# Cross attention written out straight: half of a subtraction on ScalarE, score products side by side, keys and the quantiser's last steps on GpSimd

## The chip, the cores and the metric

The program runs on one NeuronCore of one Trainium2 chip. A core has TensorE (PE: matmuls and transposes, with weight loads shown apart as PEld), VectorE (DVE), ScalarE (ACT), GpSimd (POOL) and SyncE (SP, which here only starts transfers). Every engine works through its own list of instructions in order, and semaphores join the lists. The metric is the device time of the whole program in microseconds (us); lower is better. Three runs of the kernel before gave 5644.22, 5659.84 and 5665.61 us.

## The reference, cut to what matters

The program is a chain of eight parts over x (32 sequences of 128 tokens of 128 features). The change is in the seventh, a cross attention between `seq1` = x and `seq2` = a side input, with 16 heads of 8 features:

```python
query = seq2 + b_self
key   = concatenate([seq1 + b_prev, seq2 + b_self], 1)
value = concatenate([seq1, seq2], 1)
q, k, v = query @ Wq + bq, key @ Wk + bk, value @ Wv + bv     # split into 16 heads of 8
score_prev = einsum("bhqd,bhkd->bhqk", q, k[:, :, :l1]) * SCALE
score_self = (q * k[:, :, l1:]).sum(-1, keepdims=True) * SCALE
score_prev = where(arange(l1) < seq_len1, score_prev, -inf)
weights = softmax(concatenate([score_prev, score_self], -1), axis=-1)
attn = weights[..., :-1] @ v[:, :, :l1] + weights[..., -1:] * v[:, :, l1:]
return attn @ Wo + bo
```

Each query so sees the 128 tokens of `seq1` and, of `seq2`, only its own token. What comes out is then brought to a 4-bit grid (blocks of 16 values with one 8-bit scale each, `fake_quant_nvfp4`) for the last part.

## The kernel before, in words

The layer is `level3_cond`, a block of five instruction lists. Its unit is one sequence, 32 in all, and its work is laid out by the helper `pipeline`, which gets an engine and a list of pairs (function, lag). In slot `s` the helper issues each function of the list, in the list's order, for the unit `s` minus lag. So the order of a list is the order in which an engine meets its work in a slot, and the lags say which sequence each piece is for. Before, the first slots are written out, then a loop (`Fori`) of 8 slots runs over the middle ones, then the last slots are written out.

For one sequence the work is this. TensorE projects four sequences at once (`project`: q, k, k of seq2, v by turns, one for each slot) and, with x as weights, makes the values and the own scores (`values_in`, into `m_ps`). `scores` multiplies queries by keys for 8 of the 16 heads (`half` 0 and 1) into `s_ps`; the keys lie in `k4` as four copies, in each of which all heads but one of a group of four are zeroed by the mask `hm` (function `keys`). VectorE takes the maximum over a row (`row_max`), joins it with the own score (`less_max`, first instruction) and subtracts it (`z_`). ScalarE takes the exponential (`p`), TensorE turns it (`turn_p`), ScalarE copies the turned weights out (`pT`, `keep_p`), and TensorE forms numerator and denominator in `o_ps` (`values`, 64 small products). ScalarE copies the own weight (`own_weight`, tile `owe`), GpSimd multiplies it with the own value (`own_value`, tile `tt`), VectorE divides (`join`, four instructions: `den`, `rec`, `num`, `att`), TensorE projects (`output`), and VectorE adds the bias (`finish`, into `y_tm`). All parts of `o_ps` lie in one PSUM bank: `values` of a sequence waits for `yc`, the signal of `finish` for the sequence before it.

```python
                def values(k, j, c):

                    pe.wait_ge(s_["yc"], at(k - 1))
                    pe.wait_ge(s_["owe"], at(k))
```

Once in four sequences VectorE quantises 128x512 numbers: `block_scales`, `block_values`, `block_bins` and `block_round`, 15 steps and a last product, spread over four slots by the lags 8, 9, 10 and 11. `keys` (lag 2), `shift` (two additions, lag 0) and `products` (GpSimd, lag 2) too come once in four slots.

Of the kernel before, what the change touches and what calls it, by code (L numbers as in the profile page):

```python
# [24 lines left out]
P = 128  # L25
# [39 lines left out]
def pipeline(eng, units, period, stages, k0=0, first=None, last=None, early=()):  # L65
# [3 lines left out]
    lag = max(g for _, g in stages)  # L69
    head = -(-lag // period) * period  # L70
# [1971 lines left out]
def level3_cond(nc, T, R):  # L2042
# [5 lines left out]
    with ExitStack() as ctx:  # L2048
# [25 lines left out]
        vz = m.sb("ca_vz", [P, 2, GT])  # L2074
# [4 lines left out]
        z_ = m.sb("ca_z", [P, 2, 2 * GT])  # L2079
        p = m.sb("ca_p", [P, 2, 2 * GT])  # L2080
        pT = m.sb("ca_pT", [P, 4, GT])
# [20 lines left out]
                 "top", "topo", "z", "ex", "ownz", "owe", "pT", "pTc", "oweT", "od", "owec", "t", "den", "rec",  # L2102
                 "num", "att", "y", "yc", "xstep", "xq")
# [5 lines left out]
        def diagonal(c):  # L2109

            a = vz[:, c % 2, :]
            return bass.AP(a.tensor, a.offset, [a.ap[0], [4 * 32, 4], [32 + CD, 4], [1, CD]])

        with nc.Block() as block:
            @block.sync
            def _(sp):
# [15 lines left out]
                pipeline(sp, B, 2 * GS, [(load, 0)])  # L2132

            @block.gpsimd
            def _(pool):
                m.credit(pool)
                pool.memset(vz[:, :, :], 0.0).then_inc(s_["init"], 1)
# [20 lines left out]

                def own_value(k, j, c):
# [5 lines left out]
                pipeline(pool, B, 2 * GS, [(copy_x, 0), (products, 2), (own_value, 6)])  # L2165

            @block.tensor
            def _(pe):
# [27 lines left out]
                def scores(k, c, half):  # L2196
# [3 lines left out]
                    pe.wait_ge(s_["z"], at((k - 1) * 2 + half))  # L2200
# [12 lines left out]
                def turn_p(k, c, g):  # L2213
                    pe.wait_ge(s_["ex"], at(k * 2 + g // 2))
# [6 lines left out]
                def values(k, j, c):  # L2221
# [638 lines left out]
```

## Time and profile before

| | |
|---|---|
| median of 3 runs (lowest, highest) | 5659.84 us (5644.22, 5665.61) |
| the profiled execution's own time | 5666.48 us |
| its span | 5664.7 us, 139636 instructions |
| busy over the whole span | PE 4998.9 (88%), DVE 3738.3 (66%), ACT 3349.9 (59%), POOL 3134.2 (55%) |
| the layer that is changed | from about 5091.5 to 5482.6 us in the span, 391.1 us |

The span is the time from the first to the last instruction of the profiled execution; what lies around it is 1.8 us. The changed layer is 391.1 us of it, about 7%. A busy share over the whole span says little of this layer, which is why the views below are all taken inside it. An engine's busy time counts its instructions; idle time that stands behind an instruction in brackets is what the engine waited just before it, with the instruction that ended the wait.

### The profile page before, as it was taken

What the parts mean: (1) busy time and instruction counts of PE and PEld (TensorE: products, weight loads), DVE (VectorE), ACT (ScalarE), POOL (GpSimd) and SP (SyncE); (2) the same over time, 40 slices, a digit from 0 to 9 for tenths busy, and PEclk for the clock granted to TensorE, in tenths of its full rate; (3) what the DMA queues carried; (4) which work ended last, traced back from release to release, by engine and by line L of the source; (5) the groups of instructions that cost most, each with busy time, mean ns of one, the idle gap of its engine ahead of it and who ended that gap; (6) DMA issues with size and microseconds to landing.
All of it is one profiled execution on the core that took longest, in us unless ns stands there. A gap on an engine that the chain in (4) does not pass through costs nothing. (4 is left out here: it accounts for less than half of the span.)

```text
span 5664.7 us, 139636 instructions
## 1 busy us (share of the span) xinstructions
PE 4998.9 (88%) x49540; PEld 3198.4 (56%) x49552; DVE 3738.3 (66%) x6448; ACT 3349.9 (59%) x10268; POOL 3134.2 (55%) x1457
## 2 busy tenths in 40 slices
PE   5998999457599999999999999999999999978864
PEld 1333778244366655666566656665666566634532
DVE  2111000754288968886788778876888689847888
ACT  0000000333189968996799769985999499934432
POOL 0001000112399948995799669975998499920018
PEclk9999999659699999999999999999999999988975
DMA  7767554022100000000000000000000000000000
GB/s 157 224 176 202 116 109 101 4 64 54 39 2 2 2 17 6 2 2 17 6 2 2 17 6 2 2 16 7 2 2 2 21 2 2 2 24 7 7 2 14
DMA packets 274391, 204.00 MB, mean 36 GB/s; under 512 B 179524, under 2 KB 254756, under 8 KB 267588
## 3 DMA queue, kind: packets, MB, share of 16 engines
q1 hardware_dynamic: 192924, 114.18, 8.7%
q10 hardware_dynamic: 78760, 76.68, 4.7%
q8 instruction: 433, 7.09, 0.6%
q0 software_dynamic: 2048, 4.20, 0.3%
q14 instruction: 226, 1.85, 0.1%
HBM read 131.83 MB, written 63.16 MB: 34 GB/s over the span
## 5 line engine op out<-in xcount | busy, mean ns | idle before, releaser
L1835 POOL TENSOR_TENSOR rs<-ss,minus_half 128x16 f32<-128x16 f32 x386 | 1128.1, 2923 | 106.8 <-DVE ss L1904 102.5
L1752 ACT ACTIVATE s_ps<-s_ps,low 128x128 f32<-128x128 f32 x3072 | 1059.8, 349 | 4.5
L1833 POOL TENSOR_TENSOR t<-t 128x1024 f32<-128x1024 f32 x386 | 912.2, 2363 | 128.8 <-DVE t L1893 128.8
L1840 POOL TENSOR_TENSOR qk<-t,rs 128x1024 f32<-128x1024 f32 x386 | 735.0, 1904 | 60.4 <-POOL rs L1835 23.7
L1752 ACT ACTIVATION_READ_ACCUMULATOR s_ps<-s_ps,low 128x1 f32 x3072 | 660.3, 215 | 0.0
L1887 DVE TENSOR_TENSOR t<-qk_ps,rot 128x1024 f32<-128x1024 f32 x386 | 472.3, 1224 | 178.4 <-PE qk_ps L1534 178.2
L1915 DVE TENSOR_REDUCE low<-s_ps 128x4 f32<-128x512 f32 x768 | 494.4, 686 | 123.4 <-PE s_ps L1569 122.8
L1924 DVE TENSOR_TENSOR p<-s_ps,rec 128x512 f32<-128x512 f32 x768 | 531.0, 691 | 27.0
L343 PE MATMUL l_ps<-l_core 9*128 9x512 bf16 x4096 | 443.0, 628 | 77.5 <-DMA l_core<-rows_xs 67.3
L1596 PEld LDWEIGHTS att_oT_ps<-pT,v 128*64 128x64 f32 x6144 | 328.6, 137 | 286.6 <-issue 286.6
L1766 ACT ACTIVATE pT<-pT_ps 128x512 f32<-128x512 f32 x768 | 457.1, 595 | 52.4 <-PE pT_ps L1575 43.8
L1575 PEld LDWEIGHTS pT_ps<-ident,p 128*128 128x128 f32 x3072 | 352.8, 141 | 238.7 <-issue 193.9
L1575 PE MATMUL pT_ps<-ident,p 128*128 128x128 f32 x3072 | 482.9, 280 | 0.0
L1729 ACT ACTIVATE sq<-qk_ps 128x1024 f32<-128x1024 f32 x386 | 395.9, 1026 | 140.9 <-DVE t L1893 137.2
L1901 DVE TENSOR_REDUCE ss<-sq 128x16 f32<-128x1024 f32 x386 | 466.7, 1209 | 4.8 <-ACT sq L1729 4.8
L1893 DVE TENSOR_TENSOR t<-qk_ps,rot 128x1024 f32<-128x1024 f32 x386 | 468.3, 1213 | 0.0
L1596 PE MATMUL att_oT_ps<-pT,v 128*64 128x128 f32 x6144 | 421.1, 279 | 8.8 <-issue 8.8
L1540 PE MATMUL vy_ps<-wqkv,xs 128*128 128x512 f32 x768 | 400.9, 604 | 30.8 <-issue 15.5
L1531 PE MATMUL qk_ps<-wqkv,xs 128*128 128x512 f32 x772 | 401.9, 603 | 26.7 <-DVE xs L1881 18.1
L1607 PE MATMUL vy_ps<-oT,wo 128*128 128x128 f32 x3072 | 407.7, 276 | 4.9 <-ACT oT L1778 4.9
L1534 PE MATMUL qk_ps<-wqkv,xs 128*128 128x512 f32 x772 | 397.5, 597 | 0.0
L1607 PEld LDWEIGHTS vy_ps<-oT,wo 128*128 128x128 f32 x3072 | 374.0, 192 | 7.6 <-ACT oT L1778 7.6
(400 smaller groups left out, 8560.5 us busy)
## 6 DMA issues: line engine op xcount, KB each, us to landing
l_core<-rows_xs SPq DMA_DIRECT2D x512, 72.0 KB
rows_hs<-l_core ACTq DMA_DIRECT2D x96, 384.0 KB, 6.5
z_fm<-rows_hs SPq DMA_DIRECT2D x120, 144.0 KB
x_fm<-rows_hs SPq DMA_DIRECT2D x120, 144.0 KB
wqkv<-in_wqkv SPq DMA_DIRECT2D x7, 1536.0 KB, 6.5
l_core<-rows_exs ACTq DMA_DIRECT2D x320, 18.0 KB
rows_xs<-z_fm ACTq DMA_DIRECT2D x12, 384.0 KB, 7.5
rows_exs<-l_near ACTq DMA_DIRECT2D x9, 512.0 KB, 11.7
```

The costliest lines, as they stand in the source:

```text
L1575: mm = pe.transpose(pT_ps[:, i * P:(i + 1) * P], p[:, c % 2, e, i, :], R.ident[:, :])
L1596: mm = pe.matmul(oT_ps[DH * e:DH * e + DH, i * P:(i + 1) * P], v[:, c % 8, d:d + DH], pT[:, c % 2, e, i, :], start=True, stop=True, skip_g ...
L1607: mm = pe.matmul(vy_ps[:, 0:P], wo[:, 4 * (c % UPB) + i, :], oT[:, c % 2, i, :], start=i == 0, stop=i == 3)
L1752: ins = act.activation(s_ps[:, e, i * P:(i + 1) * P], s_ps[:, e, i * P:(i + 1) * P], ACT.Exp, bias=low[:, c % 2, e, i:i + 1], scale=-1.0, ...
L1833: pool.tensor_tensor(t1[:, i, :], t1[:, i, :], t2[:, i, :], ALU.add).then_inc(s_["t12"], 1)
L1835: pool.tensor_tensor(rs[:, i, :], ss[:, i, :], R.minus_half[:, 0:2 * UH], ALU.pow).then_inc(s_["rs"], 1)
L1840: pool.tensor_tensor(qk[:, i, :].rearrange("p (h d) -> p h d", d=DH), t1[:, i, :].rearrange("p (h d) -> p h d", d=DH), rs[:, i, :].unsquee ...
L1887: dve.tensor_tensor(t1[:, i, :], qk_ps[:, :, :].rearrange("p n c -> p (n c)"), rot[:, 0, :, :, :].rearrange("p a h d -> p (a h d)"), ALU.m ...
L1893: dve.tensor_tensor(t2[:, i, :].rearrange("p (h e d) -> p h e d", e=2, d=DH // 2), swapped(), rot[:, 1, :, :, :].rearrange("p a h (e d) -> ...
L1901: dve.tensor_reduce(ss[:, i, :], sq[:, :].rearrange("p (h d) -> p h d", d=DH), AX.X, ALU.add).then_inc(s_["ss"], 1)
L1915: dve.tensor_reduce(low[:, c % 2, e, :], s_ps[:, e, :].rearrange("p (h k) -> p h k", h=4), AX.X, ALU.min).then_inc(s_[f"low{e}"], 1)
L1924: dve.tensor_tensor(p[:, i, e, :, :], s_ps[:, e, :].rearrange("p (h k) -> p h k", h=4), rec[:, i, e, :].unsqueeze(2).to_broadcast([P, 4, P ...
```

## The change

`pipeline` gets a branch: where the period is the number of units, all slots are written out and no loop is made. All five lists of the layer now go that way. In the lists, order and lags change: `join` and `finish` come one slot later (lag 8), VectorE treats the high half of one sequence (lag 6) and then the low half of the next (lag 5), and `finish` stands behind both. TensorE issues the high and the low score products one behind the other. ScalarE now gets the high half's exponential straight from the scores, in 8 instructions with the negative maximum (`minus`) as bias, in place of VectorE's subtraction and one exponential. `keys` goes to GpSimd as four products with the mask, and so do the quantiser's last three steps (`block_round`, now an addition, a subtraction and a product). `vz` gets four buffers and `pT` two. GpSimd waits for the constants before it clears its tiles.

```diff
     lag = max(g for _, g in stages)
+    if period == units:
+        for s in range(units + lag):
+            for f, g in stages:
+                if 0 <= s - g < units:
+                    f(k0 + s - g, s - g, s - g)
+        return
...
             def _(pool):
                 m.credit(pool)
+                pool.wait_ge(const, dma_at(10))
                 pool.memset(vz[:, :, :], 0.0).then_inc(s_["init"], 1)
...
+                def keys(k, j, c):
+                    if c % GS != 1:
+                        return
+                    i = (c // GS) % 2
+                    pool.wait_ge(s_["prc"], at(k))
+                    pool.wait_ge(s_["sc"], at((k - 6) * 2 + 1))
+                    for h in range(4):
+                        ins = pool.tensor_tensor(k4[:, i, :, h, :], k1[:, :].rearrange("p (b k) -> p b k", b=GS),
+                                                 hm[:, h:h + 1].unsqueeze(2).to_broadcast([P, GS, S]), ALU.mult)
+                    ins.then_inc(s_["k4"], 1)
+
+                def block_round(k, j, c):
+                    if c % GS != GS - 1:
+                        return
+                    n = k // GS
+                    pool.wait_ge(s_["xstep"], at(n * 13 + 12))
+                    pool.tensor_tensor(xvb[:, :], xva[:, :], xvm[:, :], ALU.add).then_inc(s_["xsum"], 1)
+                    pool.wait_ge(s_["xsum"], at(n))
+                    pool.tensor_tensor(xvm[:, :], xvb[:, :], xvm[:, :], ALU.subtract).then_inc(s_["xless"], 1)
+                    pool.wait_ge(s_["xless"], at(n))
+                    pool.tensor_tensor(blocks(R.xq[:, bass.ds(j * S - (GS - 1) * S, GT)]), blocks(xvm[:, :]),
+                                       over(xb8[:, :], NBX), ALU.mult).then_inc(s_["xq"], 1)
...
-                pipeline(pool, B, 2 * GS, [(copy_x, 0), (products, 2), (own_value, 6)])
+                pipeline(pool, B, B, [(own_value, 8), (copy_x, 0), (keys, 2), (products, 2), (block_round, 11)])
...
-                pipeline(pe, B, 2 * GS, [(first, 5), (turn_low, 6), (second, 5), (turn_high, 6),
-                                         (project, 1), (output, 7), (values, 6)])
+                pipeline(pe, B, B, [(turn_high, 7), (values_in, 5), (turn_low, 6), (scores_high, 6), (scores_low, 5),
+                                         (output, 8), (project, 1), (values, 7)])
...
                 def exp_high(k, j, c):
-                    exps(k, 1)
+                    act.wait_ge(s_["minus"], at(k))
+                    act.wait_ge(s_["pT"], at((k - 1) * 4 + 3))
+                    for n in range(8):
+                        ins = act.activation(p[:, 1, n * S:(n + 1) * S], s_ps[:, 2 + n // 4, n % 4, :], ACT.Exp,
+                                             bias=minus[:, c % 2, n:n + 1], scale=SCALE)
+                    ins.then_inc(s_["exh"], 1)
...
-                pipeline(act, B, 2 * GS, [(own_copy, 5), (keep_p, 6), (exp_low, 5), (projected, 1), (exp_high, 5),
-                                          (own_weight, 6)])
+                pipeline(act, B, B, [(own_weight, 8), (keep_high, 7), (keep_low, 6), (own_copy, 5), (exp_high, 6),
+                                          (exp_low, 5), (projected, 1)])
...
+                def attend_high(k, j, c):
+                    n, t, scores = halves(k, c, 1)
                     row_max(k, c, 1)
-
-                def attend_high(k, j, c):
-                    less_max(k, c, 1)
+                    own_max(k, c, 1)
+                    dve.wait_ge(s_["exh"], at(k - 2))
+                    dve.tensor_scalar(minus[:, c % 2, :], t, -SCALE, None, ALU.mult).then_inc(s_["minus"], 1)
...
-                    t(dve.tensor_tensor(xvb[:, :], xva[:, :], xvm[:, :], ALU.add))
...
-                pipeline(dve, B, 2 * GS, [(keep_v, 5), (shift, 0), (attend_low, 5), (join, 7), (max_high, 5), (finish, 7),
-                                          (attend_high, 5), (keys, 2), (masks, 4), (block_scales, 8), (block_values, 9), (block_bins, 10),
-                                          (block_round, 11)])
+                pipeline(dve, B, B, [(join, 8), (keep_v, 5), (attend_high, 6), (attend_low, 5), (finish, 8),
+                                          (shift, 0), (masks, 4), (block_scales, 9), (block_values, 10),
+                                          (block_bins, 11)])
```

VectorE before, in one of the middle slots, from the maximum of the low half to the own difference `ca_ownz` (`ca_top` is the maximum, `ca_z` the subtraction, `ca_att` the divided result, `y_tm` is `finish`):

```order
L2374 TENSOR_REDUCE ca_top<-ca_s_ps 128x8
L2379 TENSOR_TENSOR ca_top<-ca_top,ca_own 128x8
L2382 TENSOR_TENSOR ca_z<-ca_s_ps,ca_top 128x1024
L2401 TENSOR_TENSOR ca_den<-ca_o_ps,ca_owe 128x128
L2404 RECIPROCAL ca_rec<-ca_den 128x128
L2406 TENSOR_TENSOR ca_num<-ca_o_ps,ca_tt 128x128
L2410 TENSOR_TENSOR ca_att<-ca_num,ca_rec 128x128
L2374 TENSOR_REDUCE ca_top<-ca_s_ps 128x8
L2329 TENSOR_TENSOR y_tm<-ca_o_ps,ca_row 128x128
L2379 TENSOR_TENSOR ca_top<-ca_top,ca_own 128x8
L2382 TENSOR_TENSOR ca_z<-ca_s_ps,ca_top 128x1024
L2395 TENSOR_TENSOR ca_ownz<-ca_own,ca_top 128x16
```

VectorE now, in a slot of the same kind, from the last instruction of `join` on:

```order
L2377 TENSOR_TENSOR ca_vz<-ca_m_ps,ca_row 128x4x4x8
L2405 TENSOR_REDUCE ca_top<-ca_s_ps 128x8
L2410 TENSOR_TENSOR ca_top<-ca_top,ca_own 128x8
L2426 TENSOR_SCALAR ca_minus<-ca_top 128x8
L2428 TENSOR_TENSOR ca_ownz<-ca_own,ca_top 128x16
L2405 TENSOR_REDUCE ca_top<-ca_s_ps 128x8
L2410 TENSOR_TENSOR ca_top<-ca_top,ca_own 128x8
L2418 TENSOR_TENSOR ca_z<-ca_s_ps,ca_top 128x1024
L2371 TENSOR_TENSOR y_tm<-ca_o_ps,ca_row 128x128
L2387 TENSOR_SCALAR ca_xp<-x_fm,ca_col 128x512
L2388 TENSOR_SCALAR ca_sp<-side,ca_col 128x512
L2392 TENSOR_SCALAR ca_mrow<-iota,lensf 128x128
```

`y_tm` stood between the high half's maximum and its joining with the own score, with the subtraction and the own difference behind it; it now stands behind both halves, and only the mask row and the quantiser's steps are left after it. One `ca_z` is gone and `ca_minus` is there.

TensorE before, from the output projection of one slot to that of the next (`ca_o_ps<-ident,ca_oweb` and the two rows under it are `values`; `ca_m_ps<-ca_wv,ca_x` begins `values_in`):

```order
L2241 MATMUL ca_o_ps<-ca_wo,ca_att 128x128
L2225 MATMUL ca_o_ps<-ident,ca_oweb 128x128
L2230 MATMUL ca_o_ps<-ca_pT,ca_vz 32x128 x16
L2234 MATMUL ca_o_ps<-ca_pT,ca_onez 32x128 x16
L2192 MATMUL ca_m_ps<-ca_wv,ca_x 128x128
L2193 MATMUL ca_m_ps<-hind,ca_prod 128x16
L2203 MATMUL ca_s_ps<-ca_mrow,ca_onesb 128x512 x2
L2208 MATMUL ca_s_ps<-ca_k,ca_qT 128x512 x2
L2218 MATMUL ca_pT_ps<-ident,ca_p 128x128 x8
L2203 MATMUL ca_s_ps<-ca_mrow,ca_onesb 128x512 x2
L2208 MATMUL ca_s_ps<-ca_k,ca_qT 128x512 x2
L2218 MATMUL ca_pT_ps<-ident,ca_p 128x128 x8
```

TensorE now, from one `values` to the next:

```order
L2259 MATMUL ca_o_ps<-ident,ca_oweb 128x128
L2264 MATMUL ca_o_ps<-ca_pT,ca_vz 32x128 x16
L2268 MATMUL ca_o_ps<-ca_pT,ca_onez 32x128 x16
L2252 MATMUL ca_pT_ps<-ident,ca_p 128x128 x8
L2223 MATMUL ca_m_ps<-ca_wv,ca_x 128x128
L2224 MATMUL ca_m_ps<-hind,ca_prod 128x16
L2252 MATMUL ca_pT_ps<-ident,ca_p 128x128 x8
L2237 MATMUL ca_s_ps<-ca_mrow,ca_onesb 128x512 x2
L2242 MATMUL ca_s_ps<-ca_k,ca_qT 128x512 x2
L2237 MATMUL ca_s_ps<-ca_mrow,ca_onesb 128x512 x2
L2242 MATMUL ca_s_ps<-ca_k,ca_qT 128x512 x2
L2275 MATMUL ca_o_ps<-ca_wo,ca_att 128x128
```

Behind `values` there now stand the high half's turning, `values_in` and the low half's turning before a score product comes, and the two pairs of score products follow each other.

GpSimd now, in four slots of the middle, in which before there were only the rows of `ca_tt`, `ca_x` and `ca_prod` (`ca_tt` is `own_value`, `ca_k` is `keys`):

```order
L2165 TENSOR_TENSOR ca_prod<-ca_qT,ca_k 128x512
L2194 TENSOR_TENSOR ca_tt<-ca_owe,ca_v2T 128x128 x2
L2183 TENSOR_TENSOR xvb<-xva,xvm 128x512
L2185 TENSOR_TENSOR xvm<-xvb,xvm 128x512
L2187 TENSOR_TENSOR z_fm<-xvm,xb 128x512
L2194 TENSOR_TENSOR ca_tt<-ca_owe,ca_v2T 128x128
L2174 TENSOR_TENSOR ca_k<-ca_k,hm 128x4x128 x4
L2194 TENSOR_TENSOR ca_tt<-ca_owe,ca_v2T 128x128
```

The three steps of `block_round` now stand ahead of one `own_value`, and the four products of `keys` behind it.

## Rows read from the trace of the kernel before

**Rows 1.** Windows, the middle of the layer; the first line names the columns.

```profile
core 0: us, PE busy (x) PEld busy (x) DVE busy (x) ACT busy (x) POOL busy (x), PEclk, DMA share, GB/s
...
5105.10:5455.20 350.10, 288.42 (x3041) 182.64 (x3041) 287.46 (x566) 163.66 (x303) 26.58 (x42) 0.89 0.02 6
```

**Rows 2.** One line's instructions: TensorE's first product of `values_in`.

```profile
L2192 PEld LDWEIGHTS ca_m_ps<-ca_wv,ca_x x64: 186/189/338, 5104.5 to 5455.0; 128*128 128x128 f32 x64
```

**Rows 3.** Timeline of one slot: start, us, engine and line.

```profile
5288.54 1.09 PE L2218 MATMUL ca_pT_ps<-ident,ca_p 128*128 128x128 f32 x8
5288.66 1.22 DVE L2374 TENSOR_REDUCE ca_top<-ca_s_ps 128x8 f32<-128x1024 f32 x1 [0.90 <-PE ca_s_ps L2208]
5289.56 0.39 PE L2203 MATMUL ca_s_ps<-ca_mrow,ca_onesb 1*128 1x512 bf16 x2
5289.92 0.17 DVE L2379 TENSOR_TENSOR ca_top<-ca_top,ca_own 128x8 f32<-128x8 f32 x1
5290.21 1.23 DVE L2382 TENSOR_TENSOR ca_z<-ca_s_ps,ca_top 128x1024 f32<-128x1024 f32 x1
...
5294.14 0.28 DVE L2329 TENSOR_TENSOR y_tm<-ca_o_ps,ca_row 128x128 f32 x1
5294.48 0.33 PE L2225 MATMUL ca_o_ps<-ident,ca_oweb 128*128 128x128 f32 x1 [0.84 <-DVE y_tm L2329]
5294.74 1.08 PE L2230 MATMUL ca_o_ps<-ca_pT,ca_vz 128*32 128x128 f32 x32
...
5296.62 0.49 PE L2192 MATMUL ca_m_ps<-ca_wv,ca_x 128*128 128x128 f32 x2
...
5297.17 0.39 PE L2203 MATMUL ca_s_ps<-ca_mrow,ca_onesb 1*128 1x512 bf16 x2
...
5298.47 1.22 DVE L2374 TENSOR_REDUCE ca_top<-ca_s_ps 128x8 f32<-128x1024 f32 x1 [0.50 <-PE ca_s_ps L2208]
```

**Rows 4.** Timeline of TensorE at the loop's two jumps.

```profile
5227.57 0.77 PE L2192 MATMUL ca_m_ps<-ca_wv,ca_x 128*128 128x128 f32 x2 [4.14 <-issue]
5320.16 0.46 PE L2192 MATMUL ca_m_ps<-ca_wv,ca_x 128*128 128x128 f32 x2 [3.86 <-issue]
```

**Rows 5.** Groups of VectorE, 5200 to 5388 us.

```profile
L2382 DVE TENSOR_TENSOR ca_z<-ca_s_ps,ca_top 128x1024 f32<-128x1024 f32 x33 | 40.4, 1224 | 4.1 <-DVE ca_top L2379 0.7
...
L2355 DVE TENSOR_SCALAR ca_k<-ca_k,hm 128x512 f32<-128x512 f32 x16 | 6.7, 479 | 0.0
...
L2460 DVE TENSOR_TENSOR xvb<-xvb,xvm 128x512 f32<-128x512 f32 x4 | 2.7, 683 | 0.0
```

**Rows 6.** Timeline: a GpSimd product, and one VectorE instruction twice.

```profile
5273.64 1.26 POOL L2157 TENSOR_TENSOR ca_prod<-ca_qT,ca_k 128x512 f32<-128x512 f32 x1
5273.84 1.10 DVE L2429 TENSOR_SCALAR xbs<-xbs,gs 128x32 f32<-128x32 f32 x1
...
5318.15 0.24 DVE L2429 TENSOR_SCALAR xbs<-xbs,gs 128x32 f32<-128x32 f32 x1
```

**Rows 7.** Groups of GpSimd: an addition in the last part.

```profile
L2529 POOL TENSOR_TENSOR hvb<-hva,hvm 128x1024 f32<-128x1024 f32 x16 | 37.7, 2353 | 18.1 <-DVE hvm L2596 18.1
```

**Rows 8.** The page's costliest groups: exponentials of the sixth part.

```profile
L1752 ACT ACTIVATE s_ps<-s_ps,low 128x128 f32<-128x128 f32 x3072 | 1059.8, 349 | 4.5
```

**Rows 9.** Timeline of GpSimd at the layer's start.

```profile
5085.47 0.95 POOL L2137 MEMSET ca_vz<- 128x1024 f32 x1 [7.51 <-issue]
```

**Rows 10.** Timeline of TensorE at the layer's end.

```profile
5467.90 0.49 PE L2241 MATMUL ca_o_ps<-ca_wo,ca_att 128*128 128x128 f32 x2 [0.69 <-DVE ca_att L2410]
...
5473.22 0.49 PE L2241 MATMUL ca_o_ps<-ca_wo,ca_att 128*128 128x128 f32 x2 [2.24 <-DVE ca_att L2410]
```

**Rows 11.** An idle piece of TensorE, and the clock in two stretches.

```profile
5281.72 0.49 PE L2241 MATMUL ca_o_ps<-ca_wo,ca_att 128*128 128x128 f32 x2 [2.48 <-DVE ca_att L2410]
...
5280.30:5283.70 3.40, 1.14 (x19) 0.83 (x23) 3.24 (x7) 1.38 (x2) 0.00 (x0) 0.99 0.28 77
5283.70:5287.10 3.40, 3.40 (x62) 3.02 (x51) 2.80 (x8) 1.53 (x3) 0.03 (x1) 0.50 0.00 0
```

More of the change, by code:

```diff
@@ L2078, in level3_cond @@
         oweb = m.sb("ca_oweb", [P, 2, P])
-        z_ = m.sb("ca_z", [P, 2, 2 * GT])
+        z_ = m.sb("ca_z", [P, 2 * GT])
+        minus = m.sb("ca_minus", [P, 2, 8])
         p = m.sb("ca_p", [P, 2, 2 * GT])
-        pT = m.sb("ca_pT", [P, 4, GT])
+        pT = m.sb("ca_pT", [P, 8, GT])
         owe = m.sb("ca_owe", [P, 2, P])
@@ L2101, in level3_cond @@
         names = ("init", "lens", "onez", "x", "xs", "pr", "prc", "k4", "prod", "mrow", "v", "vc", "ownc", "sc",
-                 "top", "topo", "z", "ex", "ownz", "owe", "pT", "pTc", "oweT", "od", "owec", "t", "den", "rec",
-                 "num", "att", "y", "yc", "xstep", "xq")
+                 "top", "topo", "z", "minus", "exl", "exh", "ownz", "owe", "pT", "pTc", "oweT", "od", "owec", "t", "den", "rec",
+                 "num", "att", "y", "yc", "xstep", "xsum", "xless", "xq")
         s_ = {n: m.sem(f"f_{n}") for n in names}
@@ L2131, in load @@
                     sp.dma_start(side[:, i, :], T["side"][:, bass.ds(j * S, GT)]).then_inc(side_in[i], 16)
-                pipeline(sp, B, 2 * GS, [(load, 0)])
+                pipeline(sp, B, B, [(load, 0)])
             @block.gpsimd
@@ L2199, in scores @@
                     pe.wait_ge(s_["mrow"], at(k))
-                    pe.wait_ge(s_["z"], at((k - 1) * 2 + half))
+                    if half:
+                        pe.wait_ge(s_["exh"], at(k - 1))
+                    else:
+                        pe.wait_ge(s_["z"], at(k - 1))
                     for g in (2 * half, 2 * half + 1):
@@ L2241, in output, with scores_high, scores_low @@
                     pe.matmul(o_ps[:, 2, :], att[:, c % 2, :], wo[:, :], start=True, stop=True).then_inc(s_["y"], 1)
-                def first(k, j, c):
-                    values_in(k, j, c)
+                def scores_high(k, j, c):
+                    scores(k, c, 1)
+                def scores_low(k, j, c):
                     scores(k, c, 0)
-                def second(k, j, c):
-                    scores(k, c, 1)
                 def turn_low(k, j, c):
@@ L2346, in shift @@
                     dve.tensor_scalar(sp_[:, i, :], side[:, i, :], col[:, 3:4], None, ALU.add).then_inc(s_["x"], 1)
-                def keys(k, j, c):
-                    if c % GS != 1:
-                        return
-                    i = (c // GS) % 2
-                    dve.wait_ge(s_["prc"], at(k))
-                    dve.wait_ge(s_["sc"], at((k - 6) * 2 + 1))
-                    for h in range(4):
-                        ins = dve.tensor_scalar(k4[:, i, :, h, :], k1[:, :].rearrange("p (b k) -> p b k", b=GS),
-                                                hm[:, h:h + 1], None, ALU.mult)
-                    ins.then_inc(s_["k4"], 1)
                 def masks(k, j, c):
@@ L2374, in row_max, with own_max @@
                     dve.tensor_reduce(t, scores, AX.X, ALU.max).then_inc(s_["top"], 1)
-                def less_max(k, c, half):
+                def own_max(k, c, half):
                     n, t, scores = halves(k, c, half)
```

58 lines of the change are left out of this document (27 added, 31 removed).

## The prediction

> **What bounds the kernel now.** I first looked for the part of the span in which the changed layer lies and cut its middle out by windows, from the first `values_in` to the last [rows 1]. The reader is to see two things there. No engine is full: in 350.10 us of the middle PE is busy 288.42 and DVE 287.46. And the middle holds 31 intervals between the 32 `values_in` [rows 2], so one sequence costs 350.1 / 31 = 11.29 us, while the busy sums are 9.30 us (PE) and 9.27 us (DVE) a sequence. What is left over is waiting for each other, so the chain inside a slot decides, not a sum.
>
> The timeline of one undisturbed slot shows the chain [rows 3]. From one maximum of a low half (5288.66) to the next (5298.47) it is 9.81 us. DVE does maximum, joining, subtraction, then `join`, the high maximum, and at 5294.14 `y_tm`, which is `finish`. PE stands idle 0.84 us until then, since `values` of the next sequence may not overwrite the bank, and runs at 5294.48 and 5294.74 while DVE does the high half's subtraction and the rest. At 5296.62 PE begins `values_in`, at 5297.17 the low scores, and 1.30 us later DVE has them. So `finish` comes early in DVE's slot, and PE's `values` lie beside DVE's second half. That overlap is why 9.81 is possible.
>
> The difference between 9.81 and 11.29 is made by three things: slots with quantiser steps or `keys`, two stalls where PE takes the loop's jump (4.14 and 3.86 us, put down to issue [rows 4]), and stretches at half of TensorE's clock: the middle's granted clock is 0.89 on the mean [rows 1], so about 22% of it ran at 1.2 instead of 2.4 GHz.
>
> **The change, part by part.**
>
> *DVE's load.* It loses one subtraction a sequence (1.224), `keys` (4 x 0.479 once in four, so 0.48) and three quantiser steps of 0.683 or so once in four (0.51) [rows 5], and gets `minus`, priced like the joining, also 128x8, 0.17 [rows 3]. 9.27 - 1.22 - 0.48 - 0.51 + 0.17 = 7.23 us. This would be a gain of 2 us a sequence if DVE's sum decided.
>
> *The new chain of a slot.* The order rows show `finish` behind both halves, and PE's `values` still waits for it. Behind `values` PE must go through the high turning, `values_in` and the low turning before the high scores come, and DVE can't take the high maximum earlier. From `finish` round to `finish`, by starts in [rows 3]: finish to `ca_oweb` 0.34, to `values` 0.26, `values` 1.88, turning 1.02 (5288.54 to 5289.56), `values_in` 0.55, turning 1.02, scores to maximum 1.30, together 6.37 us of PE; then on DVE maximum to joining 1.26, joining 0.29, `minus` 0.17, maximum 1.26, joining 0.29, subtraction 1.23, together 4.50 us. The sum is 10.87 us. DVE's other way lies beside it and is shorter: `join` took 1.48 us (from the subtraction's end at 5291.44 to `finish` at 5294.14, less the maximum's 1.22), and ScalarE's copy ahead of it and `keep_v` behind it are one short instruction each, so some 2.3 us, where PE needs 1.02 + 0.55 + 1.02 + 1.30 = 3.9 until the high maximum can start. So the slot without extras gets slower, 10.87 against 9.81: two halves of DVE's work that PE's `values` used to cover now stand in line with it.
>
> *What is covered now.* Mask row, `shift`, scales, values and bins come after `finish`, while PE needs 0.34 + 0.26 + 1.88 and then 3.9 us. All of them cost nothing as long as they take less than about 4 us; if that cover went, `join` would be late. The slots that were 13 us long for their extras are then near 10.9.
>
> *GpSimd.* `block_round` starts when the bins are done, about 1.4 us behind `finish`, and has three instructions. The nearest row is the last part's addition of 1024 columns, 2.353 us [rows 7], so about 1.2 each and 3.6 together; its `own_value` is queued behind it and `num` waits for that, until about 5.4 us behind `finish`, where it would have been needed at 4.2. Then `keys`, four instructions of 0.95 to 1.26, run beside `join` and the high half. What such a neighbour does is seen in [rows 6]: a DVE instruction that took 0.24 us when GpSimd stood still (5318.15) took 1.10 when `ca_prod` ran, and ended with it. Bounds for a group of four sequences are 0 (all hidden in PE's 3.9 us) and 4 us; I take 1.0, since the high scores come at 6.4 us and only the delays behind them count. A mean slot is then 10.87 + 1.0 / 4 = 11.1 us.
>
> The Trainium skill, "SBUF — State Buffer", "SBUF: two separate sides", says that VectorE (in a two-port mode or with two SBUF inputs) and GpSimd take one pair of ports by an exclusive lock, for a whole instruction. The trace agrees (1.10 against 0.24 us). The rule speaks against this part of the change: by it each joining, `minus`, `ca_att` and own difference beside `keys` could wait up to one GpSimd instruction, which would put the price near the upper bound.
>
> *ScalarE.* Eight exponentials of 128x128 with a bias: the nearest row is the sixth part's, 0.349 each [rows 8], so at most 2.8 us for the eight, and they run beside the low half (1.26 + 0.29 + 1.23) and `finish`. I cost it at nothing; PE needs it only behind the next `values`, more than 2 us later.
>
> *No loop.* The two stalls of [rows 4] go, 8.0 us, and are part of the 11.29 above. The Trainium skill, "Runtime: NRT & Kernel Launch", "Instruction fetch mechanics", says that a taken branch leaves the sequential prefetch and waits for the code. The trace agrees (3.86 and 4.14 us). By it alone the time would be 8 us shorter.
>
> *Start and end.* GpSimd now clears its tiles after the constants, and twice as many `vz` (0.95 us for half of it [rows 9]): DVE and PE wait for that. Bounds are 0 (the side input lands as late) and 2.3 us (2 x 0.95 and two small fills); I take +1.7. At the end there is one slot more with nothing but `join`, `output` and `finish`, 5.3 us (5467.90 to 5473.22 [rows 10]), and the last `block_round` costs 3.6 instead of two steps of 0.7 [rows 5]: with 0.3 for the waits between, +7.8.
>
> *TensorE's clock.* The new chain leaves PE idle in every slot: from the end of the projection until `finish`, 4.84 us less the low scores (1.3), the output product (0.49 [rows 10]) and the projection (a product of the scores' width, about 1), so about 2 us in one piece. In the trace before, an idle piece of 2.48 us at `output` was followed by a stretch at half clock: 5280.3 to 5283.7 at 0.99 with PE busy 1.14, then 3.40 us at 0.50 [rows 11]. 3.4 us at half clock is 1.7 us of work lost; of PE's 9.30 us a slot 6.0 lie on the path, so 1.1 us. Bounds: no slot, or each one at 1.7 (54 us). With idle pieces as long as that one, but not all falling alike, I take two slots in three, 21 x 1.1 = 23 us.
>
> *Sum,* against the profiled execution's own 5666.5: middle 31 x (11.1 - 11.29) = -5.9; start +1.7; end +7.8; clock +23; together +26.6, so 5693. The median of the runs lies 6.6 under that execution, so the forecast for the median is 5686.5, rounded up to 5687: slower by 0.5%.
>
> **The rivals.**
>
> *Faster: DVE's relief counts.* If the scores did not have to wait for `values` (PE getting through its list earlier than I add up, so that `finish` is not behind the whole slot), PE's busy sum would decide, 9.30 us: 31 x 1.99 = -62, start and end +9.5, so 5607 for the median. For it speaks that PE and DVE are each only 82% busy; against it the wait on `yc`, which stays in the code. It decides from a slot below 10 us on. Chance 0.12.
>
> *The clock does not fall.* Idle pieces of 2 us are harmless: the rest is +3.6, so 5663.5 for the median. Against it stands [rows 11]. Chance 0.21.
>
> *GpSimd and clock both bite.* Each slot gets its half-clock stretch at the full 1.7 (+54) and the lock costs 3 us more in each of seven groups (+21), less what overlaps: about +65, 5725. Chance 0.2.
>
> *The forecast,* two thirds of the slots: 5670 to 5705, chance 0.47.
>
> **How the numbers follow.** About 0.5% (28 us) is what a measurement of this kernel can tell from no change: 5632 and 5688 are the limits. The forecast lies almost on the upper one, half of it on each side. Faster: 0.10 (the first rival less what of it is small). Slower: half of 0.47 and the 0.2, 0.43. Same: the second rival, half of the forecast and 0.02 of the first, 0.47. The range leaves out the far end of the first rival and of the third: 5638 to 5722.
>
> **What the profile after would show.** `values_in` at 10.8 to 11 us from each other at full clock; `ca_oweb` waiting about 2 us for `y_tm` in each slot; DVE idle before the high maximum, ended by the scores; `ca_tt` late once in four slots and small DVE instructions of up to 1 us beside `keys`; no wait of 4 us for issue; a granted clock of the layer clearly below 0.89. The prediction is wrong if slots are near 9 us, if the wait for `y_tm` is under 1 us, or if the clock stays at 1.

## The result and the profile after

| | before | after |
|---|---|---|
| median (lowest to highest) of 9 runs each | 5652.27 us (5644.22 to 5666.36) | 5697.74 us (5676.14 to 5721.67) |
| profiled execution: span, mean granted clock | 5664.7 us, 0.938 | 5706.2 us, 0.931 |
| middle of the layer, 31 slots | 350.5 us, 11.31 a slot | 377.1 us, 12.16 a slot |

The ratio is 1.0069, with the 95% interval 1.0049 to 1.0089: the kernel became slower, by 0.7% (the two medians of the table lie 0.8% apart).

The window of [rows 1] begins 0.6 us behind the first `values_in`, which is at 5104.5 by [rows 2]. By those rows (5104.5 to 5455.0) the middle before is 350.5 us, and all differences below go by it.

The layer's middle by windows, from the first to the last `values_in`, in the kernel after; it answers to [rows 1]:

```profile
5108.10:5485.20 377.10, 272.79 (x2968) 193.59 (x2969) 230.94 (x507) 198.69 (x509) 75.41 (x88) 0.81 0.02 6
```

DVE's busy time fell from 287.46 to 230.94 us, PE's from 288.42 to 272.79, and the stretch got 26.6 us longer. The granted clock fell from 0.89 to 0.81. The first `values_in` comes 3.5 us later (5108.0 against 5104.5), and from the last one to the last product of the quantiser it takes 38.0 us (5485.1 to 5523.1) against 27.6.

What PE waited for ahead of `ca_oweb`, in the view of that one line (us, times):

```profile
  DVE y_tm L2371: 227.7, 62
```

This counts PE and its weight load apart, so 62 times are 31 slots; before it was 55.0 us in as many. Most of the 31 slots look like the following one; about every fourth takes 13.1 to 13.6 us. PE and DVE in the timeline of the kernel after (start, us, engine, line); it answers to [rows 3]:

```profile
5306.65 0.47 PE L2259 MATMUL ca_o_ps<-ident,ca_oweb 128*128 128x128 f32 x1 [3.31 <-DVE y_tm L2371]
5307.06 1.94 PE L2264 MATMUL ca_o_ps<-ca_pT,ca_vz 128*32 128x128 f32 x32
5308.77 1.43 PE L2268 MATMUL ca_o_ps<-ca_pT,ca_onez 128*32 128x128 f32 x32
5310.13 1.09 PE L2252 MATMUL ca_pT_ps<-ident,ca_p 128*128 128x128 f32 x8
5311.06 0.39 PE L2223 MATMUL ca_m_ps<-ca_wv,ca_x 128*128 128x128 f32 x2
...
5311.56 1.12 PE L2252 MATMUL ca_pT_ps<-ident,ca_p 128*128 128x128 f32 x8
5312.61 0.41 PE L2237 MATMUL ca_s_ps<-ca_mrow,ca_onesb 1*128 1x512 bf16 x4
5312.84 1.04 PE L2242 MATMUL ca_s_ps<-ca_k,ca_qT 32*128 32x512 f32 x8
5313.81 0.49 PE L2275 MATMUL ca_o_ps<-ca_wo,ca_att 128*128 128x128 f32 x2
5314.13 1.02 PE L2213 MATMUL ca_m_ps<-ca_xp,ca_wk 128*128 128x512 f32 x2
5318.46 0.33 PE L2259 MATMUL ca_o_ps<-ident,ca_oweb 128*128 128x128 f32 x1 [3.31 <-DVE y_tm L2371]
...
5313.91 1.23 DVE L2405 TENSOR_REDUCE ca_top<-ca_s_ps 128x8 f32<-128x1024 f32 x1 [1.32 <-PE ca_s_ps L2242]
5315.53 1.22 DVE L2405 TENSOR_REDUCE ca_top<-ca_s_ps 128x8 f32<-128x1024 f32 x1
5316.98 1.22 DVE L2418 TENSOR_TENSOR ca_z<-ca_s_ps,ca_top 128x1024 f32<-128x1024 f32 x1
5318.12 0.28 DVE L2371 TENSOR_TENSOR y_tm<-ca_o_ps,ca_row 128x128 f32<-128x128 f32 x1
```

From one `ca_oweb` to the next it is 11.81 us. One after the other the reader sees `finish` (5306.32, by its 0.33 us ahead of `ca_oweb`), `values` on PE, the turnings, the scores, then 1.32 us in which DVE waits for them, then both halves on DVE and `finish` again (5318.12). PE is idle for 3.31 us at the end. Its next rows, L2264 and L2268, take 1.94 and 1.43 us; at the full clock they take 1.08 and 1.06. Of the 31 `values` after the first, 29 have one of the two rows or both above 1.4 us; the last two, behind idle pieces of 1.60 and 0.38 us, are at the full clock.

### The profile page after: what moved, and what is told of

It is laid out like the page before. It is cut to its first block and busy times, and to the rows that moved or that the text cites. A ratio compares the mean times of both kernels' runs of the same rounds, so it can differ in the third digit from the quotient of the medians.

```text
span 5706.2 us, 139290 instructions
## 1 busy us (share of the span) xinstructions
PE 4995.9 (88%) x49552; PEld 3216.8 (56%) x49552; DVE 3680.1 (64%) x6392; ACT 3389.2 (59%) x10492; POOL 3194.6 (56%) x1513
```

## The experiments

Times are medians against the kernel before on the same chip. "Middle" is the stretch from the first to the last `values_in` of the profiled execution, which is free of what happens in the rest of the program: in these profiles the first `values_in` came at any point between 5076 and 5129 us, mostly through code ahead of the layer that no experiment touches, so a small step is read from the middle rather than from one span. A middle is one execution.

| run | ratio [95%] | middle, us | clock |
|---|---|---|---|
| after | 1.0069 [1.0049, 1.0089] | 377.1 | 0.81 |
| x1: `finish` between the halves | 0.9940 [0.9919, 0.9962] | 311.5 | 0.90 |
| x2: GpSimd's new work undone | 1.0039 [1.0020, 1.0058] | 366.8 | 0.83 |
| x3: projection done three times | 1.0019 [0.9996, 1.0041] | 341.0 | 0.94 |
| x4: before, `finish` late | 1.0106 [1.0064, 1.0148] | 414.5 | 0.78 |
| x5: before, no loop | 0.9974 [0.9953, 0.9995] | 338.2 | 0.91 |
| x6: x1 and x2 together | 0.9922 [0.9898, 0.9946] | 293.9 | 0.95 |
| x7: x1, exponentials undone | 1.0018 [0.9992, 1.0044] | 341.6 | 0.86 |
| x8: x1, `keys` undone | 0.9919 [0.9893, 0.9944] | 300.7 | 0.94 |
| x9: after, scores apart | 1.0144 [1.0101, 1.0187] | 413.6 | 0.75 |
| x10: x6 again | 0.9934 [0.9911, 0.9957] | 294.4 | 0.95 |
| x11: x1, `block_round` a slot later | 0.9965 [0.9941, 0.9988] | 308.4 | 0.93 |
| x12: x1 again | 0.9948 [0.9924, 0.9972] | 311.9 | 0.90 |

The theory was that of the prediction: a ring through `finish`, and the half-clock stretch that its idle piece brings. The rivals were that GpSimd's new work (its queue and the lock) makes the time, and that the straight program or the split exponentials do.

### x1: finish between the halves

```diff
-                pipeline(dve, B, B, [(join, 8), (keep_v, 5), (attend_high, 6), (attend_low, 5), (finish, 8),
+                pipeline(dve, B, B, [(join, 8), (keep_v, 5), (attend_high, 6), (finish, 8), (attend_low, 5),
```

> The changed kernel with one edit: on VectorE, finish stands between the high and the low half instead of behind both. Theory (the slot is a ring through finish and TensorE's values): the ring loses the low half, 1.26 + 0.29 + 1.22 us, so a slot is 6.4 us of TensorE plus 1.9 of VectorE, 8.3, and then VectorE's own list (7.5 us busy and its gaps) or TensorE's decides, about 9 us; against 12.17 now that is 31 x 3.1 = 96 us less, 5600 us, and the layer's granted clock rises from 0.81 to over 0.9. Rival (GpSimd's queue and the shared ports make the slots long): the slots stay near 12 us, 5680 to 5700. Rival (ScalarE's eight exponentials are late): the same, with TensorE waiting for ca_p.

5635.4 us against 5666.62: moving one word in a list turns 0.7% slower into 0.6% faster. `finish` in the timeline of x1 (DVE, two slots), and in between PE's wait for it and what comes ahead of `values_in`:

```profile
5315.57 0.28 DVE L2371 TENSOR_TENSOR y_tm<-ca_o_ps,ca_row 128x128 f32<-128x128 f32 x1
5315.91 0.33 PE L2259 MATMUL ca_o_ps<-ident,ca_oweb 128*128 128x128 f32 x1 [0.72 <-DVE y_tm L2371]
5316.17 1.08 PE L2264 MATMUL ca_o_ps<-ca_pT,ca_vz 128*32 128x128 f32 x32
5317.06 1.06 PE L2268 MATMUL ca_o_ps<-ca_pT,ca_onez 128*32 128x128 f32 x32
5318.48 1.06 ACT L2339 ACTIVATE ca_p<-ca_z 128x1024 f32<-128x1024 f32 x1 [0.49 <-DVE ca_z L2418]
5319.44 0.67 ACT L2313 ACTIVATE ca_v2T<-ca_m_ps,ca_col 128x512 f32<-128x512 f32 x1
5320.49 0.46 PE L2223 MATMUL ca_m_ps<-ca_wv,ca_x 128*128 128x128 f32 x2 [1.35 <-issue]
5324.88 0.28 DVE L2371 TENSOR_TENSOR y_tm<-ca_o_ps,ca_row 128x128 f32<-128x128 f32 x1
```

The slot is 9.31 us, PE waits 0.72 instead of 3.31, and `values` runs at the full clock. The low half (maximum, joining, subtraction) now lies beside `values`. The middle fell by 65.6 us, where 96 were expected: the plain slot is 9.31 us and not 9, and the long ones stay.

What sets the 9.31 us now is not `finish` alone. PE stands idle 1.35 us ahead of `values_in` in the slot shown, and 28.4 us in 23 slots of the middle together. The profile puts this down to issue, but in the code `values_in` waits for the signal `prc`, and ScalarE gives it behind the low half's exponential (5318.48) and the projection's copy (5319.44 to 5320.11). So the low half seems to be still on a ring, now through ScalarE. This is read from the rows and the code; no run tests it. What remains long is one slot in four, 12.7 to 13.0 us, and in the five such slots both rows of `values` ran at 1.94 and 1.93 us; x6, x8 and x11 go into it.

### x2: GpSimd's new work undone

`keys` and `block_round` are on DVE again, as separate steps at the same lags (2 and 11).

```diff
-(own_value, 8), (copy_x, 0), (keys, 2), (products, 2), (block_round, 11)])
+(own_value, 8), (copy_x, 0), (products, 2)])
...
-(shift, 0), (masks, 4), (block_scales, 9), (block_values, 10), (block_bins, 11)])
+(shift, 0), (keys, 2), (masks, 4), (block_scales, 9), (block_values, 10), (block_bins, 11), (block_round, 11)])
```

> The changed kernel with keys and the quantiser's last three steps back on VectorE, behind finish. Theory (ring through finish): these steps lie where VectorE waits for values anyway, so the common slot stays near 11.9 us and only the long slot of each four (13.1 to 13.6 us) comes down by about 1.3 us: 8 x 1.3, and 2 us at the end, 12 us less, 5685 us. Rival (GpSimd's queue and ports are the cause of the loss): nearly the whole loss of 45 us is given back, 5655. Rival (VectorE is full): slower than 5700.

The ratio is 1.0039, and the middle shrinks by 10.3 us, to plain slots of 11.9 us. So GpSimd's part of the change costs about a third of a microsecond a slot, as expected (12 us), and the slowness stays without it: this rival is not the main cause. It is the middle that shows this; the intervals of the two ratios, x2's and after's, overlap.

### x3: the projection done three times

```diff
-                    pe.matmul(m_ps[:, :], w[:, :], x[:, i, :], start=True, stop=True).then_inc(s_["pr"], 1)
+                    for _ in range(3):
+                        mm = pe.matmul(m_ps[:, :], w[:, :], x[:, i, :], start=True, stop=True)
+                    mm.then_inc(s_["pr"], 1)
```

It adds two needless products to each slot, in the place where PE is idle.

> The changed kernel, but TensorE does each projection three times over (same operands, same result), which adds 2 us of work to every slot with a projection, all of it in the piece of 3.3 us in which it stands idle before values. Theory (idle TensorE loses its clock, and a stretch at 1.2 GHz on the ring costs 1.1 to 1.7 us a slot): the granted clock of the layer rises from 0.81 to about 0.95 and slots fall from 12.17 to about 11, 35 us less, 5662 us, although TensorE does more. Rival (the clock costs nothing, because what runs slow is hidden): 5698 or up to 10 us more.

TensorE in the timeline of x3, two `values_in` and what lies between `ca_oweb` and the scores:

```profile
5308.93 0.39 PE L2225 MATMUL ca_m_ps<-ca_wv,ca_x 128*128 128x128 f32 x2
...
5316.34 0.33 PE L2261 MATMUL ca_o_ps<-ident,ca_oweb 128*128 128x128 f32 x1 [1.59 <-DVE y_tm L2373]
5316.60 1.08 PE L2266 MATMUL ca_o_ps<-ca_pT,ca_vz 128*32 128x128 f32 x32
5317.50 1.06 PE L2270 MATMUL ca_o_ps<-ca_pT,ca_onez 128*32 128x128 f32 x32
5318.48 1.09 PE L2254 MATMUL ca_pT_ps<-ident,ca_p 128*128 128x128 f32 x8
5319.41 0.39 PE L2225 MATMUL ca_m_ps<-ca_wv,ca_x 128*128 128x128 f32 x2
...
5320.97 0.41 PE L2239 MATMUL ca_s_ps<-ca_mrow,ca_onesb 1*128 1x512 bf16 x4
```

PE does 1.7 us more in each slot, and the slot is 10.48 us instead of 11.81. Its idle piece is 1.59 us, and `values` ran at 1.08 and 1.06 us in every slot of 10.48; the half-clock rows (1.94) come only behind or in slots of over 11.7 us. By the starts, the difference of 1.33 us lies wholly in this stretch: 0.15 from `ca_oweb` to `values`, 0.81 in the first row of `values` and 0.38 in the second. This shows the price of the clock alone, and it shows the bare ring, 10.48 us. The middle fell by 36.1 us, where 35 were expected.

### x4: before, with finish late

```diff
-(join, 7), (max_high, 5), (finish, 7), (attend_high, 5), (keys, 2)
+(join, 7), (max_high, 5), (attend_high, 5), (finish, 7), (keys, 2)
```

> The kernel before with one edit: finish stands behind attend_high, not ahead of it. Theory (TensorE's values waits for finish, and the place of finish in VectorE's order is what lost the time): finish comes 2 us later in the slot and values with it, so a slot grows by 1 to 2 us, 30 to 60 us in all, 5682 to 5712 us, and the clock falls in more slots. Rival (the order is harmless, the loss came with the moved work): 5652, within 10 us.

The ratio is 1.0106, the middle 414.5 us. In the kernel before, with none of its other parts changed, moving `finish` behind the high half's joining, subtraction and own difference costs 64 us of the middle. PE's wait for `y_tm` in two neighbouring slots, from its timeline:

```profile
5289.86 0.33 PE L2225 MATMUL ca_o_ps<-ident,ca_oweb 128*128 128x128 f32 x1 [2.48 <-DVE y_tm L2329]
5290.11 1.08 PE L2230 MATMUL ca_o_ps<-ca_pT,ca_vz 128*32 128x128 f32 x32
...
5301.30 0.33 PE L2225 MATMUL ca_o_ps<-ident,ca_oweb 128*128 128x128 f32 x1 [2.48 <-DVE y_tm L2329]
5301.56 1.81 PE L2230 MATMUL ca_o_ps<-ca_pT,ca_vz 128*32 128x128 f32 x32
```

The same idle piece of 2.48 us is followed once by the full clock and once by half of it. Of the 23 such pieces in x4 (2.3 to 2.5 us), 20 were followed by a row of `values` at or near half clock. The prediction had taken two slots of three.

### x5: before, without the loop

The new branch of `pipeline` is put into the kernel before, and its five lists take it; the order of work stays.

```diff
+    if period == units:
+        for s in range(units + lag):
...
-                pipeline(dve, B, 2 * GS, [(keep_v, 5), (shift, 0), (attend_low, 5), (join, 7), (max_high, 5), (finish, 7),
+                pipeline(dve, B, B, [(keep_v, 5), (shift, 0), (attend_low, 5), (join, 7), (max_high, 5), (finish, 7),
```

> The kernel before, its pipeline written out in full instead of looping; the order of work is the same. If the loop's jumps cost what the trace of before puts down to them, the two stalls of 4.14 and 3.86 us go and the middle (first to last values_in) falls from 350.1 to about 342, by 1 to 3 us more where a stall was followed by half clock: ratio 0.9965 to 0.9985. The rival: code that runs once must be fetched all the same, so the stalls turn up elsewhere and the time is that of before, 0.9990 to 1.0010, with the middle at 348 or more.

Ratio 0.9974, middle 338.2 us, 12.3 less. Waits for issue ahead of TensorE's first product of `values_in`, in the waits of the middle (us, times, longest), first of the kernel before and then of x5:

```profile
PE ca_m_ps L2192 <- issue: 11.6, 4, 4.1
```

```profile
PE ca_m_ps L2198 <- issue: 3.5, 2, 2.6
```

8.1 of the 12.3 us are these stalls; the rest may be the clock, 0.91 instead of 0.89, but no run separates it. So the straight program is a gain by itself, and the change owes none of its slowness to it.

### x7: exponentials undone

From x1: the high half's subtraction is on DVE again, into a tile of its own, and there is one exponential.

```diff
-                    dve.tensor_scalar(minus[:, c % 2, :], t, -SCALE, None, ALU.mult).then_inc(s_["minus"], 1)
+                    dve.tensor_tensor(zh[:, :].rearrange("p (h k) -> p h k", h=8), scores,
+                                      t.unsqueeze(2).to_broadcast([P, 8, S]), ALU.subtract).then_inc(s_["minus"], 1)
```

> The kernel after with finish between the halves, and with the high half's subtraction on DVE again (one subtraction of 1024 columns into a tile of its own, one exponential), everything else as in x1. The subtraction (1.23 us) then stands ahead of finish where minus (0.17 us) stood, and finish is on the ring: the slot of 9.31 us should be 10.4, the middle 311.5 + 31 x 1.06 = 344, ratio to before 1.000 (0.997 to 1.003). The rival, that ScalarE's eight short exponentials cost as much as they save (or that the subtraction lies beside PE's work as before): 0.994 or less, the same as x1.

As forecast by the ring: the plain slot is 10.37 us instead of 9.31, which is the 1.06 of the expectation, the middle 341.6 us, the ratio 1.0018. The split exponentials are the best part of the change, 30 us of the middle in x1. What they are worth with `finish` behind both halves was not run.

### x9: scores apart

From the kernel after, on TensorE:

```diff
-(turn_low, 6), (scores_high, 6), (scores_low, 5), (output, 8), (project, 1), (values, 7)])
+(turn_low, 6), (scores_high, 6), (output, 8), (project, 1), (scores_low, 5), (values, 7)])
```

> The kernel after with its two pairs of score products no longer back to back: high scores, output product, projection, low scores. If the two pairs run side by side only when they are back to back, the low scores cost PE their own 1.2 us again, oweb's wait for y_tm falls from 3.3 to between 2 and 2.8 us, and since the low maximum comes up to 1 us later than before on DVE the slot gets 0 to 1 us longer: ratio to before 1.006 to 1.012. The rival, that the pairs don't overlap anyhow: the wait stays at 3.3 us less nothing, and the time that of after, 1.007, unless the low maximum is late.

The ratio, 1.0144, is beyond both expectations. TensorE in the timeline of x9:

```profile
5314.67 0.39 PE L2237 MATMUL ca_s_ps<-ca_mrow,ca_onesb 1*128 1x512 bf16 x2
5314.89 1.02 PE L2242 MATMUL ca_s_ps<-ca_k,ca_qT 32*128 32x512 f32 x4
5315.84 0.49 PE L2275 MATMUL ca_o_ps<-ca_wo,ca_att 128*128 128x128 f32 x2
...
5317.13 0.39 PE L2237 MATMUL ca_s_ps<-ca_mrow,ca_onesb 1*128 1x512 bf16 x2
5317.35 1.02 PE L2242 MATMUL ca_s_ps<-ca_k,ca_qT 32*128 32x512 f32 x4
5321.36 0.48 PE L2259 MATMUL ca_o_ps<-ident,ca_oweb 128*128 128x128 f32 x1 [2.99 <-DVE y_tm L2371]
5321.77 1.94 PE L2264 MATMUL ca_o_ps<-ca_pT,ca_vz 128*32 128x128 f32 x32
5323.48 1.93 PE L2268 MATMUL ca_o_ps<-ca_pT,ca_onez 128*32 128x128 f32 x32
```

One half of the scores by itself takes PE 1.17 us (5314.67 to 5315.84). Back to back the two halves together take 1.20 (5312.61 to 5313.81 in the kernel after). They lie in different 32-row parts of the array (`ca_k` 32*128, groups 0 and 1, 2 and 3), and the second half costs nothing. The low scores come 0.75 us late on DVE here, and most slots are 13.7 us; the wait for `y_tm` became 2.99 us, shorter than 3.31 but longer than the 2 to 2.8 expected. The half clock now covers all of `values` and much of the first turning (1.86 us in another slot, instead of 1.09), which my expectation had left out.

### x6, x8, x11: the long slot of x1

In x1's long slot, DVE and GpSimd in the timeline:

```profile
5301.53 0.29 DVE L2439 TENSOR_TENSOR ca_num<-ca_o_ps,ca_tt 128x128 f32<-128x128 f32 x1 [2.08 <-POOL ca_tt L2194]
5301.85 0.79 DVE L2443 TENSOR_TENSOR ca_att<-ca_num,ca_rec 128x128 f32<-128x128 f32 x1
...
5304.01 0.56 DVE L2410 TENSOR_TENSOR ca_top<-ca_top,ca_own 128x8 f32<-128x8 f32 x1
5304.60 0.97 DVE L2426 TENSOR_SCALAR ca_minus<-ca_top 128x8 f32<-128x8 f32 x1
...
5297.32 1.27 POOL L2183 TENSOR_TENSOR xvb<-xva,xvm 128x512 f32<-128x512 f32 x1 [7.94 <-DVE xvm L2486]
...
5301.04 0.46 POOL L2194 TENSOR_TENSOR ca_tt<-ca_owe,ca_v2T 128x128 f32<-128x128 f32 x1
5301.45 4.09 POOL L2174 TENSOR_TENSOR ca_k<-ca_k,hm 128x512 f32<-128x512 f32 x4
```

`ca_tt` stands behind `block_round`, and beside `keys` the small instructions take 0.79, 0.56 and 0.97 us for 0.29, 0.17 and 0.17.

x6 is x1 with the edit of x2. x8 puts only `keys` back on DVE. x11 keeps all on GpSimd and moves one lag:

```diff
-(own_value, 8), (copy_x, 0), (keys, 2), (products, 2), (block_round, 11)])
+(own_value, 8), (copy_x, 0), (keys, 2), (products, 2), (block_round, 12)])
```

> The kernel after with finish between the halves, and with keys and the quantiser's last steps on DVE again. With finish between, the plain slot took 9.31 us and one slot in four about 12.9, where GpSimd's block_round delays own_value and keys share the port with DVE. DVE's sum is then 7.23 + 0.99 = 8.22 us a sequence, under 9.31. Theory: the long slot falls to 10.5 or less, the middle from 311.5 to about 298, ratio to before 0.988 to 0.992 (against 0.994). The rival, that GpSimd relieves DVE here: the middle gets longer by the 0.99 a slot, 30 us, ratio 0.998 or more.

> The kernel after with finish between the halves, keys on DVE again, the quantiser's last three steps still on GpSimd. In x1 one slot in four took 12.9 us instead of 9.31; in it num waited 2.08 us for ca_tt behind block_round, and the rows beside keys took 0.79 (ca_att), 0.56 (joining) and 0.97 (minus) instead of 0.29, 0.17 and 0.17. If both parts count, only the second share goes and the long slot is near 12; if the lock beside keys was the whole of it, it falls to 10.3 as with both undone; if block_round was, it stays at 12.9. Ratio to before 0.992 to 0.994.

> The kernel after with finish between the halves and block_round one slot later on GpSimd, behind own_value and keys instead of ahead of them. Nothing leaves GpSimd; only own_value no longer stands behind block_round. If num's wait of 2.08 us in one slot of four is what makes that slot long, it falls from 12.9 to about 10.8, the middle from 311.5 to 297, ratio 0.990 to 0.992. The rival, that block_round's own port lock on DVE's small instructions costs as much wherever it stands: the long slot stays at 12 or more, ratio 0.994.

x6: from the fifth to the last but three, the slots are between 9.3 and 9.7 us; the middle is 293.9. x8: the long slot is 10.5 us, the middle 300.7. So `keys` on GpSimd costs 10.8 of the 17.6 us and `block_round` 6.8, the clock included; my expectation of "near 12" for x8 was too long, because with the shorter wait the clock no longer fell (0.94 in the middle). x11 refutes the idea that the queue alone counts: its middle is only 3.1 us shorter than x1's, where 14.5 were expected. The wait for `ca_tt` is gone, but DVE meets its lock in two slots now (11.4 and 10.9 us). GpSimd and two small instructions of VectorE in the timeline of x11:

```profile
5313.48 4.08 POOL L2174 TENSOR_TENSOR ca_k<-ca_k,hm 128x512 f32<-128x512 f32 x4
5317.53 1.26 POOL L2183 TENSOR_TENSOR xvb<-xva,xvm 128x512 f32<-128x512 f32 x1
...
5317.62 1.19 DVE L2426 TENSOR_SCALAR ca_minus<-ca_top 128x8 f32<-128x8 f32 x1
5320.26 1.05 DVE L2410 TENSOR_TENSOR ca_top<-ca_top,ca_own 128x8 f32<-128x8 f32 x1
```

### x10 and x12: side by side

> The same kernel as x6, beside x1's on one chip. x6 measured 0.9922 and x1 0.9940 on different chips; by the middles of their profiles (293.9 and 311.5 us) the difference is 17.6 us, 0.3%: 0.991 here if x1's again gives 0.994. If the middles don't carry over to the times, both are 0.993.

> The same kernel as x1 once more: ratio 0.994, between 0.992 and 0.996.

Both repeat: 5621.44 us (0.9934) and 5630.65 us (0.9948) on one chip, where before took 5656.1. Each is faster than the kernel before and than the kernel after. Their middles (294.4 and 311.9) repeat to 0.5 us, but the 17.5 us between them are not resolved in the times, whose intervals overlap. Which of x6, x8 and x12 is the fastest stays open; none of them shows a gain from GpSimd's new work.

## Why the prediction was right

The median, 5697.7 us, is 11 above the forecast of 5687, inside its range and on the side (slower by over 0.5%) that had 0.43. The profiled span grew by 41.5 us; the sum had 26.6. The forecast started from the 5659.84 us of three runs; against the 5652.27 of nine the median grew by 45.5 us, where 27 were forecast. By the sum's own terms:

| term | predicted | measured |
|---|---|---|
| bare ring, 31 slots | 31 x (10.87 - 11.29) = -13.0 | 31 x 10.48 - 350.5 = -25.6 |
| GpSimd's work | 31 x 0.25 = +7.8 | +10.3 (x2) |
| half clock | 21 x 1.1 = +23 | 28 x 1.33 = +37.2 |
| start and what lies ahead | +1.7 | +3.5 |
| end | +7.8 | +10.4 |

The predicted column adds up to 27.3, since the sum had rounded the slot to 11.1. The measured middle by the first three terms is +21.9, where the trace has +26.6; the other 4.7 us are in no term (one slot near the start took 14.07 us, and many plain ones 12.0 instead of 11.81). At the start, 1.7 us is that the constants landed later (5092.4 against 5090.6). The mechanism was right, but that the sum came within 15 us is in part luck: the bare ring was put 13 us too high and the half clock 14 us too low, and the two cancel.

**The ring** held in mechanism: `finish`, `values`, turning, `values_in`, turning, scores, two halves, `finish`, with DVE waiting for the scores and PE for `y_tm`. x1 cuts it in one place and takes 65.6 us off the middle; x4 makes it in the old kernel. Its length was 0.39 too large. By the rows of x3 and of after, the first turning is 0.93 us where I had 1.02, and DVE's two halves are 4.21 (5313.91 to 5318.12) where I had 4.50; there the starts of [rows 3], from which the 4.50 was added up, had lain further apart.

**The clock** was the term that was mis-sized most, and the reason is the idle piece. "Less the low scores (1.3)" took them as PE time of their own; run back to back, they lie beside the high ones (x9: 1.17 alone, 1.20 together). The idle piece is therefore 3.31 us and not about 2, and all 28 pieces of that length or more were followed by half clock, not two in three. The share was too low even for the 2.48 us that it was taken from (20 of 23 in x4). A stretch costs 11.81 - 10.48 = 1.33 us rather than 1.1. The Trainium skill, "TensorE: Matmul & The Clock Gate", "Measured speedup vs the span model", gives four row-packed tiles of K = 32 a speedup of 3.07; it was at hand and would have corrected the idle piece. The trace agrees in kind (two pairs in the time of one).

**GpSimd** was sized about right, 1.3 against 1.0 a group, inside the bounds 0 to 4. It shows little here because the slot already waits; in x1 the same work costs 17.6 us, 2.2 a group. The products of `keys` took 1.04 us each and `block_round` 1.28, 1.27 and 1.06, near what was assumed. `ca_tt` was not late once in four slots: VectorE waited for it three times in the middle, 1.9 us in all.

**ScalarE** was rightly costed at nothing: the eight exponentials took 2.18 us. **The loop**: the stalls of 4 us went as said (x5); the longest wait for issue that PE has ahead of `values_in` in after is 2.6 us.

**The end** was 2.6 us longer than forecast. One piece is in the timeline of after: the last `join` waited for `ca_tt` behind `block_round`, and PE had a further idle piece ahead of the last `values` at half clock:

```profile
5492.52 0.47 PE L2259 MATMUL ca_o_ps<-ident,ca_oweb 128*128 128x128 f32 x1 [4.17 <-DVE y_tm L2371]
5492.93 1.94 PE L2264 MATMUL ca_o_ps<-ca_pT,ca_vz 128*32 128x128 f32 x32
...
5512.96 0.29 DVE L2439 TENSOR_TENSOR ca_num<-ca_o_ps,ca_tt 128x128 f32<-128x128 f32 x1 [1.10 <-POOL ca_tt L2194]
```

**The rivals.** DVE's relief did count for nothing: 56.5 us less busy time, 26.6 us more middle. It would have, had `finish` stood elsewhere (x1 ran below the limit of 10 us a slot that the rival named). "The clock does not fall" is refuted by 0.81. "GpSimd and clock both bite" was right on the clock in nearly every slot and wrong on GpSimd, and the truth, 5697.7, lies between it and the forecast.

## What to carry to other kernels

Where two engines hand work round in a ring, find the instruction that releases the other engine and ask what stands ahead of it in its queue; its place was worth 65.6 us of the middle here, more than the 56.5 us of work taken off the engine. Then look for the next ring: in x1 it seems to run through ScalarE. Before an idle piece of TensorE is sized, check which of its products run side by side: they take away less busy time than the sum of them says. And a shortened queue on VectorE is no gain if its small instructions then meet GpSimd's products.

## What was not expected of the hardware

- Two pairs of score products in different 32-row parts took 1.20 us back to back, and one pair alone 1.17.
- Needless work made the kernel quicker: 1.7 us more of products a slot shortened it from 11.81 to 10.48 us, with the middle's granted clock at 0.94 instead of 0.81 (1.0 is 2.4 GHz, 0.5 is 1.2 GHz).
- Idle pieces ahead of `ca_oweb` of 0.72 and 1.59 us were never followed by half clock in the plain slots of x1 and x3. Those of 2.3 to 2.5 us were in 20 of 23 cases in x4, and those of 3.3 us or more in all 28 of after and in 28 of 29 in x2. The length of this one piece does not decide alone: in the last slots of x1 two of five pieces of 1.5 to 1.6 us were followed by half clock, and in x7 six of 18 of 1.7 to 1.8 us.
- VectorE's `minus`, an instruction with one tile and 8 columns, took up to 1.19 us beside GpSimd's products instead of 0.17: the lock is met by instructions with a single input tile too, as the `xbs` rows of [rows 6] had shown already.
